# A selective-scan block and a spiking layer: two additions moved from VectorE onto TensorE, and four products moved between steps

## The reference

```python
xz = x @ W_in;  xh, z = split(xz)                 # 512 + 512 channels
xc = conv3x3_depthwise(xh)
dt_r, Bp, Cp = split(xc @ W_xproj)                # 8, 16, 16
dt = softplus(dt_r @ W_dt + b_dt);  dtN = dt @ W_dtN + b_dtN
h = exp(dt * A) * h + (dtN * Bp) * xc             # scan over 2304 positions, 16 states
y = sum_n h * Cp + Dskip * xc
y = layernorm(y) * silu(z);  out = y @ W_out + b_out      # layer 0, added to x
# layer 1: images are the time axis
h1 = x @ W.T + b
v = v + (h1 - v) / 2;  s = (v >= 1);  v = v * (1 - s)     # v starts at 0; s is added to x
```

## Time and profile before

| | us |
|---|---|
| median of 3 runs | 4421.09 (4414.24 to 4431.68) |
| profiled execution | 4415.12 |
| its span, first to last instruction | 4413.4 |
| VectorE busy | 4047.4 (92%) |
| GpSimd busy | 3843.1 (87%) |
| TensorE busy | 3540.8 (80%) |
| ScalarE busy | 3411.3 (77%) |

### The profile page before, as it was taken

One profiled execution on the slowest core, in us unless ns is written; L12 is line 12 of the kernel. 1 busy time (PEld: TensorE's weight loads), 2 busy tenths in 40 slices (PEclk: granted clock), 3 DMA queues, 4 the chain that ended last, 5 costly groups with the idle time before them and its releaser, 6 DMA issues.

```text
span 4413.4 us, 64194 instructions
## 1 busy us (share of the span) xinstructions
PE 3540.8 (80%) x20244; PEld 2225.9 (50%) x20244; DVE 4047.4 (92%) x4017; ACT 3411.3 (77%) x5782; POOL 3843.1 (87%) x2518
## 2 busy tenths in 40 slices
PE   6787888888887788877888778887887788878876
PEld 3454555555555555545554555454554555445544
DVE  3999999999999999999999999999999999999996
ACT  4778787777877787777787777887787777878774
POOL 4999999889998899888999889988899888998894
PEclk8899999998999999999899999999999899999987
DMA  5233223322233223322232223222232223222310
GB/s 132 65 97 100 65 69 100 91 87 62 85 92 92 79 61 103 91 79 75 83 102 73 79 72 101 86 75 76 89 105 65 75 82 105 83 61 80 100 54 22
DMA packets 189295, 363.22 MB, mean 82 GB/s; under 512 B 27416, under 2 KB 164120, under 8 KB 188960
## 3 DMA queue, kind: packets, MB, share of 16 engines
q1 hardware_dynamic: 188960, 359.12, 27.7%
HBM read 289.84 MB, written 69.21 MB: 81 GB/s over the span
## 4 chain that ended last, share of the span: by engine, by line
DVE 26%; ACT 23%; PE 20%; issue 18%; POOL 12%; DVEq 0%; DMA 0%; POOLq 0%; ACTq 0%; SPq 0%
DVE st L1041 18%; POOL st L599 10%; PE ht L1190 8%; ACT decay L727 6%; DVE y L1017 3%; ACT L918 3%; ACT weighed L756 3%; PE work L1227 2%; ACT dt L799 2%; ACT L799 2%; PE work L1262 2%; PE work L1232 1%; PE work L1163 1%; ACT xb L878 1%; PE work L1222 1%
## 5 line engine op out<-in xcount | busy, mean ns | idle before, releaser
L1041 DVE TENSOR_TENSOR_SCAN st<-decay,st 128x1024 f32<-128x1024 f32 (+1 forms) x1536 | 2731.6, 1778 | 138.6 <-ACT decay L727 101.0
L599 POOL TENSOR_TENSOR st<-xc,bbc 128x1536 f32<-128x1536 f32 x768 | 2652.0, 3453 | 56.1 <-DMA bbc<-brow 46.9
L727 ACT ACTIVATE decay<-dt,neg_a 128x1024 f32<-128x1024 f32 (+1 forms) x1536 | 1356.8, 900 | 413.4 <-DVE st L1041 410.7
L1190 PE MATMUL ht<-ident,st 128*128 128x128 f32 x9216 | 1348.5, 297 | 337.1 <-DVE st L1041 299.9
L1190 PEld LDWEIGHTS ht<-ident,st 128*128 128x128 f32 x9216 | 1134.6, 153 | 648.8 <-DVE st L1041 465.1
L1017 DVE SCALAR_TENSOR_TENSOR y<-ht,ct,y 128x512 f32<-128x512 f32 x1536 | 1119.9, 729 | 89.8 <-PE ht L1190 89.4
L632 POOL TENSOR_TENSOR y<-y,weighed 128x512 f32<-128x512 f32 x672 | 854.4, 1271 | 340.3 <-ACT weighed L756 336.1
L756 ACT ACTIVATE weighed<-ht,ct 128x512 f32<-128x512 f32 x672 | 459.4, 684 | 274.1 <-PE ht L1190 271.7
L1227 PE MATMUL work<-xn,win 128*128 128x384 f32 x768 | 344.6, 594 | 136.7 <-DVE volt L997 103.2
L1163 PE MATMUL work<-tri,conv_w 96*32 96x384 f32 x4608 | 415.6, 493 | 5.2 <-issue 2.0
L1222 PE MATMUL work<-xn,win 128*128 128x480 f32 x768 | 359.9, 593 | 4.6 <-ACT xn L850 3.2
(11 more groups left out here) (109 smaller groups left out, 3173.2 us busy)
## 6 DMA issues: line engine op xcount, KB each, us to landing
bbc<-brow SPq DMA_DIRECT2D x192, 768.0 KB, 6.1
tri<-rows_of_xh SPq DMA_DIRECT2D x576, 200.0 KB, 3.9
rows_of_xh<-xhp SPq DMA_DIRECT2D x192, 250.0 KB, 2.4
out_dram<-ot SPq DMA_DIRECT2D x43, 384.0 KB, 4.2
xin<-in_x_dram SPq DMA_DIRECT2D x42, 384.0 KB, 3.4
st<-in_x_dram SPq DMA_DIRECT2D x6, 384.0 KB, 5.5
out_dram<-y SPq DMA_DIRECT2D x4, 384.0 KB, 2.6
brow<-xp SPq DMA_DIRECT2D x48, 24.0 KB, 1.5
```

What stands on the lines that cost most here:

```text
L599: u = g.tensor_tensor(slot, xc[:, kq % 2, :, :], bbc[:, piece_slot(kq, p), n % PIECE, :].unsqueeze(1).to_broadcast([P, DC, T]), ALU.mult)
L727: a.activation(flat(decay[:, :, :])[:, lo:hi], flat(dt[:, (k + ahead) % 2, :, :])[:, lo:hi], ACT.Exp, scale=neg_a[:, n:n + 1]).then_inc(s_ ...
L1041: v.tensor_tensor_scan(state[:, lo:hi], flat(decay[:, :, :])[:, lo:hi], state[:, lo:hi], 0.0 if h == 0 else state[:, lo - 1:lo], ALU.mult, ...
L1190: last = t.transpose(ht[:, m, c * P:(c + 1) * P], st[:, j, c, m * P:(m + 1) * P], ident[:, :])
```

## The change

1. Residual. `wo` gets one matmul ahead of its four: identity times the old `img`, in the same accumulation. VectorE's L1080 is gone; ScalarE takes the bank out, adding the bias on the way (Identity with `bias`). `wo0` and `wo1` are therefore in the late lists of steps 13 and 15; in step 13 `xh0` now comes ahead of `wo0`.
2. Statistics. `bn_stats` of half 1 moves from step 15 to the end of step 0 of the next chunk.
3. Membrane. `l` gets one matmul ahead of its two: identity times `volt`. VectorE's charge L982 is gone; bias and threshold are one number, `fire_at` = 1 - b1s; ScalarE adds `b1s` when it copies the membrane.
4. `xh` is made for the 8 rows that are new (384 columns) except in an image's first chunk; rows go to an image-high DRAM buffer, from where the convolution's copies read 10. The ScalarE copy, the write to DRAM and the normalisation (`xn`) shrink with it.
5. `TIN_STEPS` is (0, 6) instead of (6, 8).

```diff
-TIN_STEPS = (6, 8)
+TIN_STEPS = (0, 6)
-    13: ([], [(PRE2, "xh0")], [(POST, "wo0")]),
+    13: ([], [(PRE2, "xh0"), (POST, "wo0")], []),
-    15: ([(PRE, "yi1")], [], [(POST, "wo1")]),
+    15: ([(PRE, "yi1")], [(POST, "wo1")], []),
...
-                sp.dma_start(rows_v[c], xhp[:, c % 3, :, :].rearrange("p r w -> p (r w)")).then_inc(s_put[c], 16)
+                kq = (k + 1) % K
+                r0 = 0 if kq == 0 else TAPS - 1
+                sp.dma_start(rows_v[c][:, (kq * ROWS + r0) * WP:((kq + 1) * ROWS + 2) * WP],
+                             xhp[:, c % 3, r0:, :].rearrange("p r w -> p (r w)")).then_inc(s_put[c], 16)
...
+                    elif name[:2] == "wo":
+                        h = int(name[2:])
+                        xs = img[:, img_par(b, -1 if k == 0 else 0), h, (k - 1) % K * T:((k - 1) % K + 1) * T]
+                        bank_copy(name, xs, T, func=ACT.Identity, bias=bo[:, h:h + 1])
...
-                    a.activation(volt[:, h, kc * T:(kc + 1) * T], work[:, i, 0:T], ACT.Copy).then_inc(s_kept, 1)
+                    a.activation(volt[:, h, kc * T:(kc + 1) * T], work[:, i, 0:T], ACT.Identity,
+                                 bias=b1s[:, h:h + 1]).then_inc(s_kept, 1)
...
-                v.scalar_tensor_tensor(out=now, in0=now, scalar=b1s[:, h:h + 1], in1=volt[:, h, cols],
-                                       op0=ALU.add, op1=ALU.add).then_inc(s_volt, 1)
-                dve.wait_ge(s_volt, il + 1)
-                hold("dve", dve, b)
-                v.scalar_tensor_tensor(out=ob[:, h, :], in0=now, scalar=units[:, 1:2],
+                v.scalar_tensor_tensor(out=ob[:, h, :], in0=now, scalar=fire_at[:, h:h + 1],
                                        in1=img[:, img_par(b, -1), h, cols], op0=ALU.is_ge,
                                        op1=ALU.add).then_inc(s_spike, 1)
...
-                    if s in (13, 15) and post:
-
-                        h = (s - 13) // 2
-                        jw = await_filled(dve, b, k, f"wo{h}")
...
-                        v.scalar_tensor_tensor(out=xs, in0=work[:, jw, 0:T], scalar=bo[:, h:h + 1],
-                                               in1=xs, op0=ALU.add, op1=ALU.add).then_inc(emptied[jw], 1)
-                    if s in (14, 15) and post:
...
+                    if s == 14 and post:
+                        result_stats(b, k, 0)
+                    if s == 0 and POST in does(*preceding(b, k)):
+                        result_stats(*preceding(b, k), 1)
...
+                            lo = 0 if kc == K - 1 else (TAPS - 1) * W
                             for h in range(CH):
-                                last = t.matmul(work[:, i, 0:HALO], win[:, h, c * P:(c + 1) * P],
-                                                xn[:, (kc + 1) % 3, h, :], start=h == 0, stop=h == CH - 1)
+                                last = t.matmul(work[:, i, 0:HALO - lo], win[:, h, c * P:(c + 1) * P],
+                                                xn[:, (kc + 1) % 3, h, lo:], start=h == 0, stop=h == CH - 1)
...
+                            t.matmul(work[:, i, 0:T], ident[:, :],
+                                     img[:, img_par(b, -1 if k == 0 else 0), h, (k - 1) % K * T:((k - 1) % K + 1) * T],
+                                     start=True, stop=False)
                             for c in range(DC):
                                 pe.wait_ge(s_yz, q0 * DC + c + 1)
                                 last = t.matmul(work[:, i, 0:T], wo[:, c, h * P:(h + 1) * P], zs[:, c, :],
-                                                start=c == 0, stop=c == DC - 1)
+                                                start=False, stop=c == DC - 1)
...
+                            t.matmul(work[:, i, 0:T], ident[:, :], volt[:, h, kc * T:(kc + 1) * T],
+                                     start=True, stop=False)
```

67 lines of the change are left out of this document (37 added, 30 removed).

## The result

| | median, us | range of the runs | profiled span, us | mean granted clock |
|---|---|---|---|---|
| before | 4421.7 | 4414.2 to 4431.7 (4 runs) | 4413.4 | 0.922 |
| after | 4343.2 | 4340.5 to 4347.0 (4 runs) | 4340.7 | 0.926 |

The ratio is 0.9818, with a 95% interval of 0.9805 to 0.9831: 78.5 us less. Predicted were 4344 us. The sum came out; not all of its terms did.

What follows compares the result with a forecast made beforehand. VectorE was taken as the spine, with TensorE full in steps 13 to 15 of k = 1 to 3. Terms -27 - 45 + 9 - 19 + 8 - 3 = -77 us gave 4344 us; 8-in-10 range 4314 to 4388.

Steps and rivals of the forecast that it cites:

- steps 13 to 0: VectorE loses two residual additions, 1.05 us a chunk; less what TensorE and GpSimd take back, -27 us, bounds -48 and +5.
- step 8 of k=2 to 4: With the x tile gone it becomes that of the last image: 7.57 us falls to 5.35 to 5.4, together -45 us.
- steps 1 and 2: x tile statistics moved into step 1 cost +20 us; the 42 charges removed save 0.3 us each, -13 us.
- step 9: Statistics leaving save -11 us (k = 2, 3 of images 1 to 6); removed charges, their gain mostly lost to half speed, -6.
- last stage: TensorE bounds the last image's layer 1; eight instructions a pair of halves become twelve, +8 us.
- crowded chunks: k = 1 to 3, TensorE without room: about 0.1 us kept with an x tile behind, 0.5 without; -2 and -1.5 us.
- TensorE has room everywhere: Rival, 12%: chunks k = 1 to 3 keep their 1.0 us too, 20 us less, so 4324 us.
- TensorE eats the whole residual part: Rival, 18%: late ScalarE and the turns of two banks hold TensorE in k = 0, 4, 5 too; 4374 us.
- roomy chunks: k = 0, 4, 5 and image 0, TensorE with room: 27 chunks x -1.05 = -28 us; eight give back 0.6, +5.
- GpSimd takes over in k=0 and 1 as well: Rival: 16 more chunks give back 0.6 to 1 us, up to 4359 us; its chance counted within the forecast's own range.
- the stall only moves to step 0: Rival, 12%: the x tile delays step 0's transposes by 1.88 us instead of 0.4, 4375 us; with cold clock some 4390.
- slower than before: Rival, 4%: the clock falls in steps 13 and 14, about 4 us a chunk, so 4520 us.

## Why the prediction was right, term by term

The measured sums are over all steps of the two profiles; behind a slash stands the second profile of the kernel after.

| term | predicted | measured |
|---|---|---|
| steps 13 to 0 | -27, with 5 given back in k=5 | -31.7 / -32.0 there, and 0.6 us a chunk given back in k=5 |
| step 8 of k=2 to 4 | -45 | -45.2 / -45.2 |
| steps 1 and 2 (statistics +20, charges -13) | +7 | -2.8 / -2.8 |
| step 9 (statistics -11, charges -6) | -17 | -8.5 / -12.7 |
| last stage | +8 | +9.1 / +9.5 |
| step 12 | -3 | -1.2 / -1.4 |
| not in the sum: step 4 | 0 | +7.3 / +8.8 |
| step 11 | 0 | -10.0 / -5.3 |
| the other steps | 0 | +6.0 / +7.2 |
| ahead of the first scan | 0 | +4.3 / +4.8 |

**Steps 13 to 0, crowded chunks: right in mechanism and size.** The predicted 0.6 us of waiting is 0.54 more step, the predicted 0.4 in step 0 is 0.41. Two of the runs undo one of the causes of the latter each, and each takes all of it away; reordering does as well. The rival that TensorE has room everywhere falls: step 14 is full, and the doubled product counted in full. In step 14 of the kernel after weight loading is busy for 4.56 of 5.68 us and in step 13 for 3.11 of 4.68; by the Trainium skill (Perfetto Trace Analysis, Identifying the Most-Contended Engine) that would be room, and the doubled product, whose first half stands in step 13 and lengthens step 14 by 0.64, shows that there was none. The rival that TensorE eats the whole residual part falls too: taking the residual back cost 20 us.

**The roomy chunks: two errors that cancel.** k=4 was counted as roomy on the strength of the 0.76 us that `yi0` waited there. It paid 0.27 in step 14, so the residual won 0.78 there. These 0.27 us hang on the bank, which ScalarE frees. The prediction had that "some 0.2 us after both decays"; in the kernel after (image 3, k=4) the second decay ends at 2078.81, and the copy that frees the bank at 2079.40. `yi0` starts at 2079.45. Without the residual's product TensorE stands idle for it in the same chunk. ScalarE's copy in the kernel after, then TensorE's `yi0` in the kernel without the product:

```profile
2078.85 0.55 ACT L791 ACTIVATE xhp<-work 128x480 f32<-128x480 f32 x1
```

```profile
2068.37 1.16 PE L1277 MATMUL work<-skip_diag,xc 128*128 128x128 f32 x8 [0.48 <-ACT xhp L791]
```

That is why leaving the product out changed nothing in k=4, and why VectorE's residual, or `yi0` behind the transposes, took the 0.27 us away. So the step of the prediction that failed for k=4 is the time at which ScalarE frees `xh0`'s bank, 0.6 us behind the decays instead of 0.2. In k=0 the sum over steps 13 to 0 is 1.77 instead of 1.05, but not by the residual alone: half clock went away, which the prediction didn't look for, and it also went away in the kernel with the x tiles alone (0.92 us less in steps 14 and 15). Held against that kernel, the part won 0.85. Step 14 of k=0, image 3, before and then after:

```profile
1741.65:1747.06 5.41, 5.27 (x24) 4.18 (x25) 5.22 (x6) 2.65 (x6) 2.47 (x2) 0.68 0.21 82
```

```profile
1714.16:1719.48 5.32, 4.43 (x32) 3.90 (x33) 5.24 (x6) 3.87 (x9) 3.38 (x2) 1.00 0.37 149
```

The giving back in k=5 came as predicted (0.6 us, in its steps 3, 4, 5 and 8); chunk k=5 is 0.64 us shorter in image 3, 81.26 us against a forecast of "near 81.5". The last rival, that GpSimd takes over in k=0 and 1 as well, falls: steps 1 to 12 rose there by 0.10 at most.

**Step 8: right.** The last image of before was the right model, and 5.36 us the right length. The kernel with this part alone has the same 5.35. The rival that the stall only moves to step 0 is shown wrong by that kernel, whose step 0 is no longer than before.

**Steps 1 and 2: the terms nearly right, a third one missed.** A statistic costs 0.46 (0.92 for two, from two runs that move them away) and a charge 0.38 (predicted 0.3). But in before, step 1 of k=2 to 4 had run partly at the lower clock level, 0.73 in image 3, and in after it doesn't. Step 1 of k=2 there, before and then after:

```profile
1847.94:1854.35 6.41, 6.41 (x25) 3.96 (x24) 6.38 (x9) 5.05 (x13) 6.33 (x5) 0.73 0.11 41
```

```profile
1818.55:1825.47 6.92, 6.24 (x32) 4.19 (x32) 6.73 (x9) 6.04 (x15) 6.84 (x6) 1.00 0.11 39
```

That is some 0.2 to 0.3 us a chunk, since the step rose by 0.23 to 0.37 and not by 0.92 - 0.38 = 0.54.

**Step 9: the term that came out short.** Of the predicted 17 us it gave 8.5 or 12.7, by profile. The profiles don't say which half failed. The statistics, predicted with 0.93 in k=2 and 3, gave 0.88 and 0.62 in the kernel with that part alone, and putting them back cost 0.15 and 0.90. "Half speed costs the second fire most of its gain" kept 0.3 of 0.53 us for the charge; the run with the charge back shows 0.01 in k=2 and 3 against one profile of the kernel after, 0.10 and 0.24 against the other. What is plain is k=1, where only the charge could win: step 9 got no shorter at all. TensorE, then VectorE's first fire, in step 9 of k=1, image 3 of the kernel after the earlier trace rows:

```profile
1774.62 1.65 PE L1296 MATMUL work<-volt,ident 128*128 128x384 f32 x2 [1.34 <-ACT dt L809]
1776.06 2.48 PE L1299 MATMUL work<-img,w1s 128*128 128x384 f32 x4
1778.38 0.81 PE L1296 MATMUL work<-volt,ident 128*128 128x384 f32 x2
1779.03 1.45 PE L1299 MATMUL work<-img,w1s 128*128 128x384 f32 x4
...
1778.68 0.62 DVE L996 SCALAR_TENSOR_TENSOR ob<-work,fire_at,img 128x384 f32<-128x384 f32 x1 [2.59 <-PE work L1299]
```

The first half of `l` is six instructions here. They take 3.92 us (1774.62 to 1778.54), the six of the second half 2.10, the identity product alone 1.65 and 0.81: that is the price of starting behind a gap. The fire waits 2.59 us for them. The prediction saw this effect for the second fire and put nothing on the first. That this is what ate the gain is read from the timeline; no run isolates it.

**The clock was the blind spot.** The prediction asked whether it would fall in steps 13 to 15 and took it as given elsewhere. In images 1 to 6 it didn't fall there: 1.00 in every one of these steps of the kernel after. In image 0 it did, in step 14 of k=0 (0.73). So the rival "slower than before" is out; its price, about 4 us a chunk, was less than its own numbers give (3.35 for `wo0` and 2 more). In fact the stretches at half clock moved: into step 4, out of steps 11 and 1 and out of step 14 of k=0. Image 3 of before and after: step 4 of k=4, and step 11 of k=1.

```profile
2057.16:2062.37 5.21, 4.22 (x42) 2.60 (x42) 4.87 (x5) 4.19 (x10) 3.75 (x3) 1.00 0.61 166
...
1814.74:1820.68 5.94, 5.94 (x23) 4.14 (x22) 5.43 (x6) 5.53 (x8) 4.78 (x5) 0.71 0.00 0
```

```profile
2020.25:2026.96 6.71, 5.82 (x30) 4.17 (x34) 5.03 (x5) 4.18 (x9) 3.74 (x3) 0.52 0.68 177
1786.08:1791.42 5.34, 5.34 (x28) 3.70 (x27) 5.34 (x6) 5.28 (x8) 5.03 (x5) 1.00 0.00 0
```

The first cost 1.50 us and the second gained 0.60, in steps that have the same instructions in both kernels. The unpredicted terms are +18 and -10 in the first profile, +21 and -5 in the second (5 of the plus being the giving back in k=5); of the known ones, steps 1 and 2 came out 10 better and step 9 4 to 9 worse. That the forecast missed the median by 1 us only is in part luck. The Trainium skill (TensorE: Matmul & The Clock Gate, HAM oscillation) ties the slow state to gaps of idleness; the rows above agree that it comes behind such a gap, and add that the same gap of 2.31 us doesn't always bring it.

**What stays open.** Which of the gaps is followed by half clock, and why it was all 18 with the statistics in step 9, was not found: gaps of 2.31 us were followed by it in 7 to 18 of 18 steps, by kernel. Whether the 0.28 us by which the change lengthens the gap brought the rise from 3 to 10 is open too: with the charge back, and so with 2.03 us, it was in 8. Why the first scan is 4 to 5 us late in the kernel after is open too; products ahead of it ran at the lower level in other places (a convolution of 24 in 3.58 us, at the upper one 2.14), but no run isolated that.

## What to carry to other kernels

Where an engine is full, as TensorE was from step 13 to 0, price an edit by its start-to-start time there and expect the parts of a change to overlap: here the one part gave 42 us alone and 26 beside the others, and a reordering gives something only if nothing that is wanted soon stands behind the work that goes last. A wait that vanishes at the spine is worth its length only as far as the next engine's lateness (0.76 us moved out of step 7 came back to the hundredth in step 8). And before a saving of under 1 us a chunk is claimed, look at the granted clock behind every gap of the matmul engine: when work left step 1 here, the clock was at its lower level in all 18 profiled steps 4, three steps on, and the gain was gone.

## What the runs showed of the hardware that was not expected

- The level of the clock behind a gap: with the same instructions and the same 2.31 us of idle TensorE, step 4 took 5.21 us or up to 6.71; the lower level was in 7, 10, 11 (the second profile of the same kernel), 12, 15, 16 or 18 of 18 such steps, by kernel, and in 3 or 8 where the gap was 2.03 us. Between two profiles of one kernel single steps of this kind differ by over 1 us, while steps 13 to 2, at the upper level, repeat to 0.01 in images 1 to 6.
- An identity product of 384 columns costs TensorE 0.64 to 0.67 us in a full row of work (0.81 by its length, two instructions), and that alone was worth 11 us in steps 14 and 0 when removed and 35 when added (14 and 41 in the whole time): the price of the same instruction depends on which side of the edge the engine stands.
- ScalarE's copy of a 128x384 bank takes 0.569 us with a bias (Identity) and 0.486 without (Copy).
